# Feed-forward stages by halves of the tokens, with resident split weights and expert shares through DRAM

## The reference

```python
x = x + attention(layernorm(x))          # 16 heads, TISA bias
x = x + ffn(layernorm(x))                # stage f1
x = x + mamba(layernorm(x))
x = x + ffn(layernorm(x))                # stage f2, the same weights

def ffn(x):                              # H 128, 64 experts of 64, two shared blocks of 128
    scores = sigmoid(xf @ router_w.T)
    sfc = scores + correction_bias
    # 8 groups of 8 experts: the sum of a group's two best picks 4 groups; in them the 8 best experts
    tw = scores of these / their sum * 2.5
    combine = zeros(T, 64).at[token, expert].add(tw)
    routed = sum over e: combine[:, e] * (relu(xf @ up_w[e])**2 @ down_w[e])
    shared = relu(xf @ shared_up_w)**2 @ shared_down_w
    return routed + shared
```

## Time and profile before

| | us |
|---|---|
| time, median of 3 runs (lowest, highest) | 1184.79 (1184.17, 1186.43) |
| the profiled execution | 1184.06 |
| its span in the profile | 1182.1 |
| attention stage | 0 to 502.5 |
| f1: head, units and tail | 502.5 to 544.6, 544.6 to 766.6 |
| Mamba stage | 766.6 to 920.4 |
| f2: head, units and tail | 920.4 to 962.5, 962.5 to 1182.1 |
| busy over the span: PE, DVE, ACT, POOL | 1020.0, 983.5, 719.0, 447.7 |

### The profile page before, as it was taken

One profiled execution on the slowest core, in us unless ns is written; L12 is line 12 of the kernel. 1 busy time (PEld: TensorE's weight loads), 2 busy tenths in 40 slices (PEclk: granted clock), 3 DMA queues, 4 the chain that ended last, 5 costly groups with the idle time before them and its releaser, 6 DMA issues. The chain is left out here.

```text
span 1182.1 us, 19693 instructions
## 1 busy us (share of the span) xinstructions
PE 1020.0 (86%) x5756; PEld 540.9 (46%) x5756; DVE 983.5 (83%) x2432; ACT 719.0 (61%) x1175; POOL 447.7 (38%) x404
## 2 busy tenths in 40 slices
PE   3559999999999999785999999782877769999998
PEld 1212222222222222264766676541656537666775
DVE  6589999889999986168999999787876689999997
ACT  5116665666666656564777777586333537777775
POOL 4600000000000000013777778515663127777776
PEclk9659999999999999967999999986889879999999
DMA  3740122032012200000000000000000000000001
GB/s 100 255 95 8 61 76 49 16 106 66 15 55 75 57 1 2 1 21 12 20 21 18 22 18 23 3 19 0 1 0 0 21 9 21 22 18 21 19 23 38
DMA packets 56704, 41.66 MB, mean 35 GB/s; under 512 B 23334, under 2 KB 51004, under 8 KB 56636
## 3 DMA queue, kind: packets, MB, share of 16 engines
q1 hardware_dynamic: 54268, 38.18, 12.0%
q10 hardware_dynamic: 2368, 2.63, 0.8%
HBM read 33.12 MB, written 7.47 MB: 34 GB/s over the span
## 5 line engine op out<-in xcount | busy, mean ns | idle before, releaser
L514 POOL TENSOR_TENSOR f_act_low<-f_act,f_act_high 128x512 fp32r<-128x512 f32 x256 | 331.2, 1294 | 151.3 <-ACT f_act_high L471 146.3
L1203 ACT ACTIVATE at_prob<-at_cols 128x1024 f32<-128x1024 f32 x256 | 248.1, 1021 | 198.4 <-PE at_cols L1092 198.4
L1255 DVE CUSTOM_DVE_ANT_0 at_rows<-at_rows,at_table_max 128x512 f32<-128x512 f32 x512 | 340.3, 719 | 33.5 <-PE at_rows L1057 32.3
L471 ACT CAST f_act_high<-f_act 128x512 fp32r<-128x512 f32 x256 | 159.1, 621 | 68.1 <-DVE f_act L591 65.7
L585 DVE TENSOR_TENSOR f_gated<-f_relu,f_work 128x512 f32<-128x512 f32 x256 | 174.3, 681 | 21.3 <-PE f_work L417 15.1
L591 DVE TENSOR_TENSOR f_act<-f_gated,f_work 128x512 f32<-128x512 f32 x256 | 175.8, 687 | 10.2
L478 ACT ACTIVATE f_relu<-f_work 128x512 f32<-128x512 f32 x256 | 152.9, 597 | 32.1 <-PE f_work L362 30.7
L360 PE MATMUL f_work<-f_x_high,f_wu_high 128*128 128x512 f32 x256 | 148.4, 580 | 2.7 <-DVE f_wu_low L573 2.1
L1057 PE MATMUL at_rows<-at_k_stack,at_q_stack 48*128 48x512 bf16 x512 | 104.7, 405 | 39.9 <-DVE at_maxima L1255 38.4
L1104 PE MATMUL at_pv<-at_prob,at_v_stack 128*32 128x512 f32 x1024 | 136.4, 605 | 0.6 <-ACT at_prob L1203 0.6
L1092 PE MATMUL at_cols<-at_table_cols,flip_sum 128*64 128x512 f16 x1024 | 136.4, 387 | 0.0
(11 more groups left out here) (274 smaller groups left out, 1393.8 us busy)
## 6 DMA issues: line engine op xcount, KB each, us to landing
at_table_cols<-bias_rows SPq DMA_DIRECT2D x32, 248.0 KB, 5.1
at_table_max<-bias_rows SPq DMA_DIRECT2D x12, 480.0 KB, 4.3
f_wu<-in_L_ffn_up_w_dram SPq DMA_DIRECT2D x64, 64.0 KB, 2.0
f_wd<-in_L_ffn_down_w_dram SPq DMA_DIRECT2D x64, 64.0 KB, 1.8
at_q_stack<-q_parts SPq DMA_DIRECT2D x28, 96.0 KB, 2.4
at_k_stack<-k_parts SPq DMA_DIRECT2D x24, 96.0 KB, 3.9
at_table_max<-bias_rows ACTq DMA_DIRECT2D x4, 480.0 KB, 5.8
k_parts<-at_parts SPq DMA_DIRECT2D x2, 768.0 KB, 5.4
```

The lines of the kernel that those rows point to most:

```text
L471: nc.scalar.copy(act_h[:, j % 4, :], act[:, j % 4, :]).then_inc(act_high, 1)
L514: nc.gpsimd.tensor_tensor(act_l[:, k, :], act[:, k, :], act_h[:, k, :].bitcast(F32), ALU.subtract).then_inc(act_low, 1)
L1203: act(prob[:, S % 2, 2 * hp:2 * hp + 2, :], s2[:, hp, :, :], ACT.Exp).then_inc(exp_done, 1)
L1255: nc.vector.tensor_tensor_reduce(out=slot, in0=slot, in1=t_max[:, 2 * p.hp + j, c:c + BANK][:, ::-1], scale=1.0, scalar=-3.0e38, op0=ALU.a ...
```

## The change

**Halves.** The 16 tiles are taken in two halves of 8 tiles, two quarters each. A half's units are now a shared block or pair times two quarters: 34 x 2 = 68. The head of half 0 stands alone; the head of half 1 is written as a generator that is woven between the units of half 0, by step numbers (`AT_...`): such a number says before the end of which unit the step is put in the queue of its engine. The tail of half 0 is woven into half 1 in the same way. Loops are unrolled.

**Units.** A share goes in as its root: `act = square(relu(hid) * root)`. DVE has one operation (relu and times `cw`, L590), ACT a square and the high part, POOL the low part (L475), PE six matmuls (L379, L386). `relu`, the spread matmul and the constant are gone. The hidden PSUM tile has two banks where it had three, and `act_high`/`act_low` six slots where they had four. Shared units take a `max` with 0 on DVE.

**Shares.** The root is ACT's Sqrt followed by one Newton step on DVE (L566 to L574: max, reciprocal, times, plus, half). It is transposed on PE (128 columns, expert and quarter in partitions), copied to `rcT` and written to DRAM by SP (L316, `c_rows`). From there two DMAs for each pair (L326), one for each expert, put its row of 512 tokens of two quarters on 64 partitions, 256 KB each, into one of four slots of `cw`. SP waits for the gates of the pair four before.

**Weights.** All weights are loaded once, in the attention stage (SP, nine steps, 256 KB and 256 KB each, the first with the shared ones), and split there by POOL: four operations of 128x512 each for a step. They stay in SBUF for both stages. For room, the raw buffers share memory with other tiles of the attention stage, and in Mamba `raw` holds one sequence where it held two, so that ACT's copy for the second waits for DVE's convolution of the first; `yg` shares memory with `sz`. The constants `ident16` and `spread`, a memset and three selects on POOL, are gone.

The core of the diff:

```diff
+NPAIRS = SHARED + PAIRS
+HALVES = 2
+TH = T // HALVES
+HT = NT // HALVES
+QH = NQ // HALVES
+FFN_UNITS = NPAIRS * QH
+C_SLOTS = 4
+ACT_SLOTS = 4
+PART_SLOTS = 6
+LAG = 4
...
+def allot_weights(m):
+    m.wu_h, m.wu_l = (m.sb(f"wu_{k}", [D, NPAIRS, P], F32R) for k in ("high", "low"))
+    m.wd_h, m.wd_l = (m.sb(f"wd_{k}", [P, NPAIRS, D], F32R) for k in ("high", "low"))
...
+def weave(main, side):
...
+    side = iter(side)
+    due = next(side, None)
+    for k, _ in enumerate(main):
+        while due is not None and due <= k + 1:
+            due = next(side, None)
+    while due is not None:
+        due = next(side, None)
...
+AT_ROOT, AT_ROWS, AT_TURN, AT_COPY, AT_HIGH, AT_LOW, AT_LOGITS = 2, 3, 5, 6, 7, 8, 8
+AT_SCORE, AT_ROUTE = 12, 13
+AT_C_ROOT, AT_NEWTON, AT_C_TURN, AT_C_COPY = 38, 39, 42, 43
+AT_TAIL = 8
...
+        def sp_shares(sp, b):
+            h = halves[b]
+            sp.wait_ge(h.rcT_ready, 1)
+            sp.dma_start(c_rows[QH * b:QH * (b + 1)].rearrange("q e t -> (q e) t"), rcT[:]).then_inc(h.rc_out, 16)
+            sp.wait_ge(h.rc_out, 16)
+            for k in range(PAIRS):
+                if k >= C_SLOTS:
+                    sp.wait_ge(h.gate_done, QH * (SHARED + k - C_SLOTS + 1))
+                elif b:
+                    sp.wait_ge(halves[0].gate_done, QH * (NPAIRS - C_SLOTS + k + 1))
+                for e in range(2):
+                    src = c_rows[QH * b:QH * (b + 1), 2 * k + e, :].unsqueeze(0).broadcast_to([HID, QH, BANK])
+                    sp.dma_start(cw[HID * e:HID * (e + 1), (k + b * PAIRS) % C_SLOTS, :, :], src).then_inc(h.c_in[k % C_SLOTS], 16)
+                yield
+                yield
...
+        def pe_units(pe, b):
+            h = halves[b]
+            def up(n):
+                pp, cols = n // QH, slice((QH * b + n % QH) * BANK, (QH * b + n % QH + 1) * BANK)
+                if n == 0:
+                    pe.wait_ge(h.x_low, QH)
+                    if b:
+                        pe.wait_ge(halves[0].gate_done, FFN_UNITS)
+                if n >= 2:
+                    pe.wait_ge(h.gate_done, n - 1)
+                for k, (w, x) in enumerate(((m.wu_h, xh), (m.wu_h, xl), (m.wu_l, xh))):
+                    last = nc.tensor.matmul(hid[:, n % 2, :], w[:, pp, :], x[:, cols], start=(k == 0), stop=(k == 2))
+                last.then_inc(h.up_done, 1)
...
+            def down(n):
+                pp, s = n // QH, n % PART_SLOTS
+                pe.wait_ge(h.low_done, n + 1)
+                for k, (w, x) in enumerate(((m.wd_h, act_h), (m.wd_h, act_l), (m.wd_l, act_h))):
+                    last = nc.tensor.matmul(acc[:, QH * b + n % QH, :], w[:, pp, :], x[:, s, :],
+                                            start=(pp == 0 and k == 0), stop=(pp == NPAIRS - 1 and k == 2),
+                                            skip_group_check=True)
+                last.then_inc(h.down_done, 1)
+            for n in range(FFN_UNITS + LAG):
+                if n < FFN_UNITS:
+                    up(n)
+                if n >= LAG:
+                    down(n - LAG)
+                yield
...
+                a.wait_ge(h.square_done, n + 1)
+                if n >= PART_SLOTS:
+                    a.wait_ge(h.down_done, n - PART_SLOTS + 1)
+                elif b:
+                    a.wait_ge(halves[0].down_done, FFN_UNITS)
+                nc.scalar.copy(act_h[:, n % PART_SLOTS, :], act[:, n % ACT_SLOTS, :]).then_inc(h.high_done, 1)
+            for n in range(FFN_UNITS):
+                a.wait_ge(h.gate_done, n + 1)
+                if n >= ACT_SLOTS:
+                    a.wait_ge(h.low_done, n - ACT_SLOTS + 1)
+                elif b:
+                    a.wait_ge(halves[0].low_done, FFN_UNITS)
+                nc.scalar.activation(act[:, n % ACT_SLOTS, :], gated[:, n % 3, :], ACT.Square).then_inc(h.square_done, 1)
+                if n:
+                    high(n - 1)
+                yield
+            high(FFN_UNITS - 1)
...
+            v.wait_ge(h.root_ready, 1)
+            ch.link(ts(sfc[:], root[:], 1e-18, None, ALU.max))
+            ch.link(nc.vector.reciprocal(sfc[:], sfc[:]))
+            yield AT_NEWTON + 1
+            ch.link(tt(sfc[:], sfc[:], masked[:], ALU.mult))
+            ch.link(tt(sfc[:], sfc[:], root[:], ALU.add))
+            yield AT_NEWTON + 2
+            if b:
+                v.wait_ge(halves[0].rcT_done, 1)
+            ts(rc[:].rearrange("p k a e -> p a k e"), sfc[:].rearrange("p (a k) e -> p a k e", a=QH), 0.5, None,
+               ALU.mult).then_inc(h.rc_ready, 1)
...
+        def dve_units(v, b):
+            h = halves[b]
+            for n in range(FFN_UNITS):
+                v.wait_ge(h.up_done, n + 1)
+                if n >= 3:
+                    v.wait_ge(h.square_done, n - 2)
+                elif b:
+                    v.wait_ge(halves[0].square_done, FFN_UNITS)
+                if n < SHARED * QH:
+                    ins = nc.vector.tensor_scalar(gated[:, n % 3, :], hid[:, n % 2, :], 0.0, None, ALU.max)
+                else:
+                    k = n // QH - SHARED
+                    v.wait_ge(h.c_in[k % C_SLOTS], 32 * (k // C_SLOTS + 1))
+                    ins = nc.vector.scalar_tensor_tensor(out=gated[:, n % 3, :], in0=hid[:, n % 2, :], scalar=0.0,
+                                                         in1=cw[:, (k + b * PAIRS) % C_SLOTS, n % QH, :], op0=ALU.max, op1=ALU.mult)
+                ins.then_inc(h.gate_done, 1)
+                yield
...
+        def stage_program(head, units, tail, eng):
+            run(head(eng, 0))
+            weave(units(eng, 0), head(eng, 1))
+            weave(units(eng, 1), tail(eng, 0))
+            run(tail(eng, 1))
...
-                def unit(i, j):
-                    slot = j // 4 % 2
-                    if j % 4 == 0:
-                        pe.wait_ge(w_low, 6 * i + (j // 4 + 1))
-                    if past(i, j, 3):
-                        pe.wait_ge(act_ready, BODY * i + (j - 2))
-                    up(wu_h[:, slot, :], wu_l[:, slot, :], j % 4, j)
-                    if past(i, j, LAG):
-                        down_routed(i, j - LAG)
-                    if past(i, j, 1):
-                        pe.wait_ge(gate_done, BODY * i + j)
-                    e = 12 * i + 2 * (j // 4)
-                    mm(cw, m.spread[:, bass.ds(e, 2), :].rearrange("p e j -> p (e j)"),
-                       cT[:, (j % 4) * BANK:(j % 4 + 1) * BANK], start=True, stop=True).then_inc(cw_done, 1)
-                each_unit(pe, unit)
...
-                    if past(i, j, 2):
-                        a.wait_ge(gate_done, BODY * i + (j - 1))
-                    nc.scalar.activation(relu[:, j % 2, :], hid[:, j % 3, :], ACT.Relu).then_inc(relu_ready, 1)
...
-                        slot = (j // 4 + 1) % 2
-                        a.wait_ge(up_in[slot], 48 * i + 16 * ((j // 4 + 1) // 2 + 1))
-                        a.wait_ge(w_low, pair)
-                        nc.scalar.copy(wu_h[:, slot, :], wu[:, slot, :]).then_inc(w_high, 1)
...
-                    v.wait_ge(relu_ready, BODY * i + (NS + j + 1))
-                    v.wait_ge(cw_done, BODY * i + (j + 1))
-                    if past(i, j, 2):
-                        v.wait_ge(act_ready, BODY * i + (j - 1))
-                    tt(gated[:, j % 2, :], relu[:, j % 2, :], cw, ALU.mult).then_inc(gate_done, 1)
-                    v.wait_ge(gate_done, BODY * i + (j + 1))
-                    if past(i, j, 4):
-                        v.wait_ge(act_low, BODY * i + (j - 3))
-                    else:
-                        v.wait_ge(down_done, NS + j - 3)
-                    tt(act[:, j % 4, :], gated[:, j % 2, :], hid[:, j % 3, :], ALU.mult).then_inc(act_ready, 1)
-                    if j % 4 == 0 and past(i, j, 4) and not (isinstance(i, int) and pair + 1 == PAIRS):
-                        low_part(wu, wu_h, wu_l, (j // 4 + 1) % 2, w_high, pair + 2, w_low)
-                    if j % 4 == 1:
-                        low_part(wd, wd_h, wd_l, j // 4 % 2, wd_high, pair + 1, wd_low)
...
+                    if S in WEIGHT_STEPS:
+                        k = WEIGHT_STEPS.index(S)
+                        if k >= 2:
+                            sp.wait_ge(raw_low, 2 * (k - 1))
+                        load_weights(sp, k)
...
+                    pool.wait_ge(raw_in[k % 2], 32 * (k // 2 + 1))
+                    for a, (high, low) in enumerate(((m.wu_h, m.wu_l), (m.wd_h, m.wd_l))):
+                        src = raw[:, k % 2, a, 0:n].rearrange("p (n d) -> p n d", d=P)
+                        nc.gpsimd.tensor_copy(high[:, cut, :], src).then_inc(raw_high, 1)
+                        pool.wait_ge(raw_high, 2 * k + a + 1)
+                        tt(low[:, cut, :], src, high[:, cut, :].bitcast(F32), ALU.subtract).then_inc(raw_low, 1)
+                for S in range(ALL_STEPS):
+                    if S % STEPS == 0 and S >= STEPS and S // STEPS + 1 < ITERS:
+                        pool.wait_ge(pv_done, S)
```

(11 more changed lines are left out.)

626 lines of the change are left out of this document (304 added, 322 removed).

## The result

The changed kernel takes 1167.87 us (median of 4 runs, 1164.49 to 1170.84) beside 1184.88 for the kernel before on the same chip: a ratio of 0.985, 95% interval 0.983 to 0.987. It is **1.5% faster**, where I had forecast 1187.5 and 0.2% slower. The time lies in the range, at its lower end, on the side of rival A.

A forecast was written before the change was run, and what follows sets the result against it. PE was taken to bound the routed units; gains of 22.7 and 18.95 us less 42 (X twice), 1.4 (Mamba) and 1.0 (attention) gave -2.75, so 1187.5 us (1145.5 + 2X), range 1167 to 1213.

The forecast's parts named there:

- rival A: Woven head of half 1: side work overlaps, X 10.5 to 18, total 1166.5 to 1181.5 us; chance 0.32.
- the Mamba term: Mamba stage: ACT's raw copies wait for DVE's convolution, delaying the dt chain; 1.4 us lost, 0 to 4.8.
- The unit: Routed feed-forward units: six matmuls take 1.395 us, PE still last, POOL close behind at 1.34.
- The head: Start of a feed-forward stage, eight tiles before half 0: first routed gate 41 to 42 us after the start.
- Attention: Attention stage: POOL's added weight splits and SP's loads cost 1.0 us, 0 to 6.
- X: Cost in half 0 of half 1's woven head, mainly DVE and POOL excluding each other: 21 us a stage, 10.5 to 34.
- The rest of a stage: Feed-forward stage from first routed gate to last down, without the woven head's cost: units, refill between halves, uneven end.
- stray work: Half 1 of a feed-forward stage: PE's transposes of tail 0 and logits add 2 us.
- the seam: Between the two halves of a feed-forward stage: the pipeline runs out and fills again, 5.65 us.
- The feed-forward stages: Both feed-forward stages: gains of 22.7 - X and 18.95 - X us, against X of 21 in each.
- Rival B: Shares' loads to 64 partitions bind half 1, up to 3.45 us a pair; total 1195 to 1217; chance 0.16.
- Rival C: DVE and POOL alternate, some 35 two-input operations each waiting; X 27 to 34, total 1199.5 to 1213.5; chance 0.12.

The follow-up runs named there:

- unrolled: The kernel before with the change's Mamba part and its feed-forward unit and weight-load loops unrolled, Mamba's own loops kept: 1175.24 us, ratio 0.991.
- before: The kernel before the change, unedited, the base of the ratios: 1184.88 us on the same chip.
- mamba_part: The kernel before with only the change's Mamba part (raw with one sequence, ACT's wait, yg in sz's memory): 1187.25 us, ratio 1.0015.

## Why the prediction was wrong, point by point

The step that failed is the Mamba term with what stood behind it: "1.4 taken, 0 to 4.8" as a loss, and nothing at all for the unrolling, of which the change says only "Loops are unrolled". The stage became 6.8 us shorter, 8.2 off, and the runs put that down to the unrolling. Two terms of the feed-forward stages were mis-sized besides, by 4.7 and 6.9 us in all. Each of the three errors went the same way.

- **The unit**: 1.395 forecast, 1.397 measured. Right. POOL is busy 56.0 of 60 us in the steady units, 93% where I had 95%.
- **The head**: first routed gate 41.5 forecast, 41.4 measured. Right, the reciprocal too (3.3 and 3.35).
- **Attention** +1.0, measured +1.2 in this execution; the kernel before and its forms gave 502.1 to 504.4 for it, the changed kernel and its forms 503.8 to 506.4. In the range; between executions it varies by more than the term.
- **X**: 18.5 and 18.8 for 21, which is 4.7 us over both stages. The exclusion of DVE and POOL is shown, its size was off: the routing cost 7.5 with all that stands in it, also a wait of 1.72 for the sigmoid, where I had summed 11 for the two-input operations (the root's among them; the trace has seven of 512 columns, not eight, which changes their sum little). The Newton stretch cost 7.5 and 6.6 where I had 2.7 and a part of ACT's 3: I had placed the reciprocal but not the wait for the root right ahead of it. Units 4 to 12 cost 3.6 and 4.7; their gates wait for PE, at whose transposes and logits I had put only a part of 2.
- **The rest of a stage**: from the first routed gate to the last down, less X, I had 197.05; measured are 193.1 in f1 and 192.8 in f2. The terms in f1, forecast and measured: from the first routed gate to the end of its low part 5.2 and 5.1; the other 63 units, less X, 87.9 and 87.3; from the last low part of half 0 to the first of half 1 5.65 and 5.66; half 1 from there to its last low part 93.5 with 2 of stray work, and 93.9; to the last down 0.7 with 2.1 for an uneven end, and 1.0. So the seam was right. Of the 4.1 for stray work and an uneven end most did not come: the gates of half 1 show 1.9 over the steady rate, its low parts only 0.3, and the end is even. With the heads and tails 3 us and 4 us less.
- **Mamba**: forecast +1.4, measured -6.8. The edit alone costs 0.6 in its stage, so the term was about right for what it priced. Unrolling the loops of the feed-forward stages, made together with Mamba's part, takes the kernel from 1.0015 to 0.991 of before, and the Mamba stage from 153.3 to 145.6. **With Mamba's part it is some 10 of the 17 us by which the changed kernel is faster.**
- **The feed-forward stages** were to lose 0.3 us in all and gained 11.3. Unrolling gives little of it: `unrolled` has 525.7 us for both together, the changed kernel 515.5, and `before` 526.9. The ratios of 0.991 and 0.985 leave 7 us for the rest of the change, since the attention stage takes 1.3 us back and single executions differ by some us.
- The sum: 4.7 for X, 6.9 for the rest of the stages, 8.2 for Mamba, less 0.2 for attention: 19.5 us.
- **Rival A** gave the time, but by luck: with X at 18.65, the mean, the recorded 1145.5 + 2X is 1182.8, and the other 15 us come from terms that A did not name. The root and the reciprocal were not swallowed, at 7.5 and 6.6. **Rival B** fell. A pair's 512 KB came in 2.79 us, 188 GB/s in windows of 60 us, and the gates waited for PE; the 152 GB/s of the earlier trace rows was no limit for these loads. **Rival C** named the right wait but a price that was not reached: eleven operations waited for POOL, not some 35.

Why the unrolled stages ahead make Mamba faster is open. The first and the last of its 16 operations `ss_Ht` on DVE, one for each chunk, start 72.2 us apart in `before` and 72.1 in `mamba_part`, 65.7 in `unrolled` and 66.1 in the changed kernel, so most of it is in the chunks. The thirteen profiles with unrolled feed-forward stages have 145.6 to 150.4 us for the stage, the three with loops 152.7 to 153.8. From the start of the chunks on the windows are (`before`, then `unrolled`):

```profile
837.00:920.50 83.50, 61.96 (x346) 50.56 (x346) 61.47 (x165) 26.05 (x63) 40.84 (x52) 0.90 0.00 0
```

```profile
835.30:911.60 76.30, 57.46 (x346) 46.36 (x346) 62.91 (x167) 26.97 (x66) 44.08 (x53) 0.96 0.00 0
```

PE is busy 4.5 us less, at a granted clock of 0.96 for 0.90. Whether the clock is a cause of the shorter chunks or comes with them is not separated. That a small shift in when the engines begin decides it is a guess; no run tried it by itself.

## What to carry to other kernels

When side work is woven into a full pipeline, look at each operation's form and not only at its length: with two SBUF inputs it can wait for a busy POOL's operation to end (eleven did here, up to 1.1 us each), with an input in PSUM it did not. Keep a piece of side work shorter than the slack, and place a step that waits for another engine two or three units after the step that feeds it. Look at the outermost dimension of a DMA's pattern on both sides (64 ran at full rate here, 2 did not), and price what a change does to untouched stages by making it alone: unrolling (some 10 us), memory layout (7 to 11) and the seam between two loops (2.9 a stage) were each of the order of what the feed-forward stages gained by the edit that the change was named for (10 beside `unrolled`).

## What the runs showed of the hardware that I had not expected

- A single-input TENSOR_SCALAR between SBUF tiles, 64 columns, took 1.24 us beside POOL and 0.23 with its tiles in PSUM.
- Matmuls of 512 columns at the full granted clock followed each other every 0.233 or 0.227 us, by the addresses of tiles of the stage in SBUF alone.
- A load whose source had 2 outermost ran at 50 GB/s; with 64 it ran at 188 or more.
- 153.3 or 145.6 us for the same Mamba code with the same instructions, by whether the stages around it had loops.
